# A graph layer's start and end: table stored in pieces, preparation less far ahead, sums in two banks, division on ScalarE

## The reference

```
w_m = (efeat @ W_msg + b_msg).reshape(E, 16, 16)
w_a = (efeat @ W_attn + b_attn).reshape(E, 16, 16)
e1 = w_m * x[src][:, :, None];  e2 = w_a * x[src][:, :, None]
ex = exp(e2 - segment_max(e2, dst)[dst])
ft = segment_sum(e1 * ex / segment_sum(ex, dst)[dst], dst)
out = layernorm(x + ft.sum(axis=1))
```

## Time and profile before

| what | us |
|---|---|
| median of 3 runs | 1687.11 (1686.28 to 1688.92) |
| the profiled execution, its own time | 1689.2 |
| its span, first to last instruction | 1687.1 |
| PE, DVE, ACT, POOL busy | 1308.6, 1514.4, 987.8, 966.8 |
| span of the loop by the shifts of tiles 0 and 109 | 179.77 to 1547.51 |
| the nodes' five pieces on DVE | 1618.34 to 1678.02 |

### The profile page before, as it was taken

How to read it: one execution, slowest core, us unless ns; L and a number is a source line. 1 busy time by engine, 2 the same in 40 slices (tenths; PEclk the granted TensorE clock), 3 DMA queues, 4 the chain that set the end, 5 groups by cost and what they waited for, 6 DMA issues and landing times. The chain is left out here.

```text
span 1687.1 us, 20610 instructions
## 1 busy us (share of the span) xinstructions
PE 1308.6 (78%) x5657; PEld 675.5 (40%) x5657; DVE 1514.4 (90%) x1504; ACT 987.8 (59%) x2062; POOL 966.8 (57%) x878
## 2 busy tenths in 40 slices
PE   0002799999999999999999999999999999998300
PEld 0001444444444444444444444444444444443200
DVE  8623899999999999999999999999999999998368
ACT  1002567767767767777777677677676666664100
POOL 5777777777676767677677777676770000000170
PEclk9999899999999999999999999999999999999655
DMA  4314344444444444444444444444443223221250
GB/s 109 81 19 106 89 131 122 128 128 118 133 125 115 132 126 119 128 125 119 130 122 124 129 118 131 125 116 133 125 118 115 88 79 99 84 75 51 62 149 15
DMA packets 175870, 182.93 MB, mean 108 GB/s; under 512 B 48376, under 2 KB 131208, under 8 KB 175758
## 3 DMA queue, kind: packets, MB, share of 16 engines
q1 hardware_dynamic: 141838, 158.74, 30.0%
q0 software_dynamic: 33920, 22.89, 9.5%
HBM read 92.36 MB, written 89.41 MB: 108 GB/s over the span
## 5 line engine op out<-in xcount | busy, mean ns | idle before, releaser
L490 POOL DMA_INDIRECT split<-x_parts,edge_src x784 | 873.1, 1114 | 321.5 <-issue 221.6
L797 PE MATMUL bank_sum<-em,row_onehot 128*128 128x512 f32 x1760 | 861.6, 602 | 31.0 <-ACT sum_rows L661 31.0
L1031 DVE TENSOR_TENSOR em<-bank_prod,h_rows 128x1024 f32<-128x1024 f32 x440 | 515.7, 1213 | 41.8 <-issue 32.6
L797 PEld LDWEIGHTS bank_sum<-em,row_onehot 128*128 128x128 f32 x1760 | 307.5, 189 | 269.4 <-issue 235.2
L1049 DVE TENSOR_TENSOR em<-em 128x1024 f32<-128x1024 f32 x220 | 267.8, 1218 | 3.5 <-ACT em L620 3.5
L785 PE MATMUL bank_prod<-w_rows,partsT 100*128 100x512 bf16 x880 | 269.5, 388 | 1.5 <-DVE em L1031 1.5
L1074 DVE TENSOR_TENSOR em<-em,bank_max 128x2048 f32<-128x2048 f32 x110 | 250.7, 2279 | 3.2 <-ACT node_max L652 3.2
L661 ACT COPY sum_rows<-bank_sum 128x512 f32<-128x512 f32 x220 | 126.6, 576 | 176.6 <-PE bank_sum L797 176.6
L620 ACT ACTIVATE em<-em 128x2048 f32<-128x2048 f32 x110 | 210.5, 1913 | 1.5 <-DVE em L1074 1.4
L644 ACT COPY chunk_fwd<-bank_max 128x512 f32<-128x512 f32 x110 | 64.5, 586 | 238.0 <-PE bank_max L727 238.0
L490 POOL DMA_INDIRECT em<-sums,rec_from_i x4 | 4.0, 992 | 305.2 <-DMA sums<-sum_rows 304.3
(11 more groups left out here) (166 smaller groups left out, 1214.6 us busy)
## 6 DMA issues: line engine op xcount, KB each, us to landing
sums<-sum_rows SPq DMA_DIRECT2D x110, 512.0 KB, 3.0
rec<-split_records SPq DMA_DIRECT2D x220, 144.0 KB, 2.2
split_records<-split SPq DMA_DIRECT2D x97, 288.0 KB
mask<-tile_table SPq DMA_DIRECT2D x110, 192.0 KB, 3.3
split<-x_parts,edge_src POOLq DMA_INDIRECT x784
rel<-tile_table SPq DMA_DIRECT2D x110, 64.0 KB, 3.0
edge_feat<-in_features SPq DMA_DIRECT2D x97, 64.0 KB
flag<-tile_table SPq DMA_DIRECT2D x110, 2.0 KB
```

The costliest lines, as they stand in the source:

```text
L490: return nc.gpsimd.indirect_dma_start(out, None, src, bass.IndirectOffsetOnAxis(idx, 0))
L797: mm = nc.tensor.matmul(bank_sum[:, :], row_onehot[:, t % RING, g, :], em[:, t % RING, s * GROUPS + g, :, :, :].rearrange("p i m o -> p (i ...
L1031: V.tensor_tensor(em[:, v, 2 * j:2 * j + 2, :, :, :].rearrange("p s i m o -> p s i (m o)"), bank_prod[j % 2][:, :, :].rearrange("p s (i x) ...
```

## The change

- **Table.** `c_tab` is stored in three pieces, `rel` first, then flags, then masks; DVE computes them in this order, with a semaphore for each. SP loads the records of tiles 0 and 1 and the flags of tile 0 between the pieces, ahead of the loop; the masks' piece stands in iteration -2. The record table is stored in iteration 0 and loaded in iteration 2, before both were earlier. The transposed row counts use `bank_sum`, and `base_row` is copied as soon as it is turned.
- **Preparation.** PREP_FIRST is 4 and not 6, so LEAD is 8. The loads of preparations 5 and 6, which stood ahead of the table's load on SP, now stand in iterations -4 and -3.
- **Last sums.** The second group of tiles 108 and 109 goes to `bank_t[1]`, and the waits for the copies allow one group more.
- **Nodes.** ACT computes a guess exp(-ln(s)) of each 1/s; DVE makes s*guess and m*guess and then (s*guess - 2)*(m*guess), which is -m/s after one Newton step; the mask for nodes is negated. ACT runs a first Sqrt on one element behind the last Exp.

```diff
-PREP_FIRST = 6
+PREP_FIRST = 4
+        def sums_bank(t, g):
+            return bank_t[1] if t >= TILES - 2 and g == 1 else bank_sum
...
             store_prep(0)
-            load_prep(5)
             store_prep(1)
-            load_prep(6)
...
-            sp.wait_ge(chunk_ready, 1)
-            sp.dma_start(tab_d, c_tab[:, :]).then_inc(tab_stored, 16)
...
-            for q in range(2, PREP_FIRST - 2):
-                store_prep(q)
+            sp.wait_ge(rel_ready, 1)
+            sp.dma_start(tab_d[:, 3 * WIDE:4 * WIDE], c_tab[:, 3 * WIDE:4 * WIDE]).then_inc(rel_stored, 16)
...
+            load_records(0)
+            sp.wait_ge(flags_ready, 1)
+            sp.dma_start(tab_d[:, 4 * WIDE:8 * WIDE], c_tab[:, 4 * WIDE:8 * WIDE]).then_inc(flags_stored, 16)
+            load_records(1)
+            load_flags(0)
             for t in range(FIRST, LAST + 1):
                 load_prep(q + 1)
-                load_records(t + 4)
+                if t + 4 > 1:
+                    load_records(t + 4)
+                if t == -2:
+                    sp.wait_ge(masks_ready, 1)
+                    sp.dma_start(tab_d[:, 0:3 * WIDE], c_tab[:, 0:3 * WIDE]).then_inc(masks_stored, 16)
...
+            for c in range(5):
+                act.wait_ge(f_loaded[c], 80)
+                guess = f_guesses[0:NODE_P, c % 2, :, :, :]
...
+                since(act, f_used, c - 1)
+                nc.scalar.activation(guess, whole[:, :, :, 0, :], ACT.Ln).then_inc(f_log, 1)
+                act.wait_ge(f_log, c + 1)
+                nc.scalar.activation(guess, guess, ACT.Exp, scale=-1.0).then_inc(f_guess, 1)
+            nc.scalar.activation(f_stat[:, 3, 0:1], eps[:, :], ACT.Sqrt)
...
-                    since(pe, sums_copied, 2 * t + g)
+                    since(pe, sums_copied, 2 * t + g - 1 if t >= TILES - 1 or (t == TILES - 2 and g == 1) else 2 * t + g)
                 for s in slots:
-                    mm = nc.tensor.matmul(bank_sum[:, :], row_onehot[:, t % RING, g, :],
+                    mm = nc.tensor.matmul(sums_bank(t, g)[:, :], row_onehot[:, t % RING, g, :],
...
             for c in range(5):
-                v_eng.wait_ge(f_loaded[c], 80)
-                link(V.reciprocal(sums_of(c, 0), sums_of(c, 0)))
-                link(V.tensor_tensor(sums_of(c, 1), sums_of(c, 1), sums_of(c, 0), ALU.mult))
+                v_eng.wait_ge(f_guess, c + 1)
...
+                link(V.tensor_tensor(sums_of(c, 0), sums_of(c, 0), guess, ALU.mult))
+                link(V.tensor_tensor(sums_of(c, 1), sums_of(c, 1), guess, ALU.mult))
+                link(V.scalar_tensor_tensor(out=sums_of(c, 1), in0=sums_of(c, 0), scalar=2.0, in1=sums_of(c, 1),
+                                            op0=ALU.subtract, op1=ALU.mult))
```

More of the change, by code:

```diff
@@ L128, in gnn_kernel @@
         has_edges = sb("has_edges", [P, NODE_COLS])
+        minus_edges = sb("minus_edges", [P, NODE_COLS])
         table = sb("table", [TILES, WIDE, COLUMNS])
@@ L224, in gnn_kernel @@
         fin = region(0, NODE_COLS, BOTH)
+        guess_at = NODE_COLS * BOTH
+        f_guesses = em_flat[:, guess_at:guess_at + 10 * ATT].rearrange("p (u n i o) -> p u n i o", u=2, n=5, i=FEAT)
         iotas = sem("iotas")
@@ L240, in gnn_kernel @@
         ends_ps = sem("ends_ps")
-        chunk_ready = sem("chunk_ready")
+        rel_ready = sem("rel_ready")
+        negrow_ready = sem("negrow_ready")
+        flags_ready = sem("flags_ready")
+        masks_ready = sem("masks_ready")
+        records_ready = sem("records_ready")
         chunk_ps = sem("chunk_ps")
+        base_copied = sem("base_copied")
         chunk_cols = sem("chunk_cols")
-        tab_stored = sem("tab_stored")
+        rel_stored = sem("rel_stored")
+        flags_stored = sem("flags_stored")
+        masks_stored = sem("masks_stored")
         rectab_stored = sem("rectab_stored")
@@ L308, in gnn_kernel @@
         f_loaded = [sem(f"f_loaded{c}") for c in range(5)]
+        f_log = sem("f_log")
+        f_guess = sem("f_guess")
         f_used = sem("f_used")
@@ L407, in load_records @@
                 q = min(t, PREPS - 1)
+                sp.wait_ge(base_copied, 1)
                 sp.wait_ge(split_stored[q % PREP_RING], rounds(q, PREP_RING))
@@ L421, in load_flags @@
                 w = t % 2
+                sp.wait_ge(flags_stored, 16)
                 since(sp, h_ready, t - 1)
@@ L452, in _ @@
                 if t == 0:
+                    sp.wait_ge(records_ready, 1)
+                    for k in range(4):
+                        sp.dma_start(rectab_d[k, :].rearrange("(t r) -> t r", r=4),
+                                     c_rec[:, k, :]).then_inc(rectab_stored, 16)
+                if t == 2:
                     sp.wait_ge(rectab_stored, 64)
@@ L573, in _ @@
                 part3(q - 2)
-            act.wait_ge(chunk_cols, 3)
             def row_places(t):
@@ L579, in row_places @@
                     return
+                act.wait_ge(chunk_cols, 2)
                 since(act, sums_ready, 2 * (t - RING + 1))
@@ L660, in copy_sums @@
                     act.wait_ge(rows_stored[v], 16 * (t // OUT_RING))
-                nc.scalar.copy(sum_rows[:, v, g, :], bank_sum[:, :]).then_inc(sums_copied, 1)
+                nc.scalar.copy(sum_rows[:, v, g, :], sums_bank(t, g)[:, :]).then_inc(sums_copied, 1)
             for t in range(FIRST, LAST + 1):
@@ L686, in _ @@
             nc.scalar.activation(r_weight[:, :, :], r_shift[:, :, :], ACT.Exp).then_inc(r_exp, 1)
+            for c in range(5):
+                act.wait_ge(f_loaded[c], 80)
+                guess = f_guesses[0:NODE_P, c % 2, :, :, :]
+                whole = fin[0:NODE_P, 5 * c:5 * c + 5, :].rearrange("p n (i m o) -> p n i m o", m=2, o=FEAT)
+                since(act, f_used, c - 1)
[3 more added lines that the diff above has]
+            nc.scalar.activation(f_stat[:, 3, 0:1], eps[:, :], ACT.Sqrt)
             act.wait_ge(f_var, 1)
@@ L908, in _ @@
             V.tensor_copy(w_part[:, 2, :], w_rest[:, :]).then_inc(w_split, 1)
-            for q in range(PREP_RING):
+            for q in range(PREP_FIRST - 1):
                 rest1(q)
@@ L921, in _ @@
             link(V.tensor_tensor(has_edges[:, :], start[:, 1:COLS], start[:, 0:NODE_COLS], ALU.is_gt))
+            link(V.tensor_scalar(minus_edges[:, :], has_edges[:, :], -1.0, None, ALU.mult))
             link(V.tensor_scalar(tmp[:, :], start[:, :], 1.0, 0.0, ALU.subtract, ALU.max))
@@ L964, in _ @@
             link(V.tensor_copy(tile_carry[:, :], bank_max[0:TILES, 128:128 + COLUMNS]))
-            link(V.tensor_scalar(c_node[:, :], filled[:, 0, :], tile_carry[:, 0:1], None, ALU.max))
             link(V.tensor_scalar(c_off[:, :], filled[:, 1, :], tile_carry[:, 1:2], None, ALU.max))
-            link(V.tensor_scalar(c_begin[:, :], filled[:, 2, :], tile_carry[:, 2:3], None, ALU.max))
             link(V.tensor_tensor(c_blk[:, :], chunk_iota[:, :], c_off[:, :], ALU.subtract))
             link(V.tensor_scalar(c_blk[:, :], c_blk[:, :], float(NUM_BLOCKS - 1), None, ALU.min))
[L970 to L974, removed]
+            link(V.tensor_scalar(c_base[:, :], c_blk[:, 0:WIDE:P], float(LAST_BASE), None, ALU.min))
+            V.tensor_tensor(c_tab[:, 3 * WIDE:4 * WIDE].rearrange("t (g j) -> t g j", g=GROUPS),
+                            c_blk[:, :].rearrange("t (g j) -> t g j", g=GROUPS), bc(c_base[:, :], 2, [TILES, GROUPS, P]),
+                            ALU.subtract).then_inc(rel_ready, 1)
+            v_eng.wait_ge(rel_ready, 1)
+            link(V.tensor_scalar(c_begin[:, :], filled[:, 2, :], tile_carry[:, 2:3], None, ALU.max))
             link(V.tensor_tensor(c_at[:, :], c_begin[:, :], c_group[:, :], ALU.max))
-            link(V.tensor_tensor(c_negrow[:, :], c_group[:, :], c_at[:, :], ALU.subtract))
+            V.tensor_tensor(c_negrow[:, :], c_group[:, :], c_at[:, :], ALU.subtract).then_inc(negrow_ready, 1)
+            v_eng.wait_ge(chunk_ps, 1)
+            V.tensor_copy(base_row[:, :], bank_t[0][0:GROUPS, 0:TILES]).then_inc(base_copied, 1)
             for col, out in ((3, c_first), (4, c_end)):
@@ L984, in _ @@
                 link(V.tensor_scalar(c_a[:, :], c_first[:, :], float(k), None, ALU.is_gt))
-                link(V.scalar_tensor_tensor(out=c_tab[:, (4 + k) * WIDE:(5 + k) * WIDE], in0=c_end[:, :], scalar=k + 0.5,
-                                            in1=c_a[:, :], op0=ALU.is_lt, op1=ALU.add))
+                flags = V.scalar_tensor_tensor(out=c_tab[:, (4 + k) * WIDE:(5 + k) * WIDE], in0=c_end[:, :], scalar=k + 0.5,
+                                               in1=c_a[:, :], op0=ALU.is_lt, op1=ALU.add)
+                if k < SLOTS - 1:
+                    link(flags)
+            flags.then_inc(flags_ready, 1)
+            v_eng.wait_ge(flags_ready, 1)
+            link(V.tensor_scalar(c_node[:, :], filled[:, 0, :], tile_carry[:, 0:1], None, ALU.max))
             link(V.tensor_tensor(c_a[:, 1:WIDE], c_node[:, 1:WIDE], c_node[:, 0:WIDE - 1], ALU.not_equal))
```

(2 more changed lines are left out.)

29 lines of the change are left out of this document (13 added, 16 removed).

## The result

The change made the kernel faster. The median of four runs is 1649.72 us (1646.35 to 1650.12), against 1687.94 of the kernel before in the same comparison (1686.28 to 1688.92): a ratio of 0.977, 95% interval 0.9753 to 0.9787. The forecast was 1649 in 1641 to 1658. The profiled execution took 1650.12, its span 1648.2, so 38.9 us less span than before.

The account below looks back on a forecast made before the run. Bounds: PE and DVE in the loop, POOL's preparations at the start, DVE's reciprocals at the end. Gains 19.0 + 3.0 + 16.1 = 38.1 off 1689.2 give 1651.1, less 2.1 for the median: 1649, range 1641 to 1658.

Parts of the forecast that it names:

- The tile does not change: Loop over the tiles: PE and DVE keep 12.57 us a tile, and two preparations moved into it cost nothing.
- The start, 19.0: Before tile 0's shift: shorter lead and table in three pieces bring it from 179.77 to 160.8, 19.0 us, range 15 to 21.
- store_prep(5) waits for POOL, about 150.7: SP's iteration -1: the store of preparation 5 waits for POOL until about 150.7; tile 2's flags end at 151.8.
- the prediction's two ways: Tile 0's shift: 159.5 counted from tile 2's flags, 160.3 to 161.3 over tile 1's flags and the forward scan.
- The sums, 3.0: Last sums in two banks: three boundaries lose their wait, 1.0 us each, 3.0 us; lower bound 2.3.
- The tail, 16.1: Node pieces: POOL's gathers become the bound in place of DVE; end at 1661.9 against 1678.0, 16.1 us.
- the gathers' delay: Tail: nine DVE two-input operations fall on POOL's gather issue and delay it 0 to 3.4 us, 2.5 taken.
- the last landing: Tail: 5.78 us from the fifth gather's start to landing, taken from the first piece, puts piece 4 at 1648.6.
- Rival 1: Start: it does not move, as a piece's landing or preparation 5's late load can hold the flags; 1668, chance 0.08.
- Rival 2: Tail: each gather waits for a whole DVE two-input operation, three pieces 13.4 us late in place of 2.5; 1660, chance 0.08.
- Rival 3: Loop: the shorter lead makes every tile wait; at 0.5 us a tile the time is 1704, chance 0.03.
- the terms' own bounds: Ranges behind 1641 to 1657: start 15 to 21, sums 2.3 to 3.2, tail 13 to 20 us.

Follow-up runs that it names:

- the faster version: Changed kernel with flags of tiles 1 and 2 moved ahead on SP, no Newton step, node pieces of 6, 6, 6, 4 and 3: 1642.29 us.
- the kernels that took one half back: Changed kernel with preparation six tiles ahead again (PREP_FIRST 6), 1668.03 us; changed kernel with the table stored whole ahead of everything, 1655.2 us.
- the part alone: Kernel before with only the second bank for the last sums added: 1685.17 us, ratio 0.998, against 1688.4.

## Why the prediction was right

- **The tile does not change.** Forecast 12.57, measured 12.57 with a lead of 10, 8 and 7. The two preparations more in the loop cost nothing.
- **The start, 19.0.** Measured 18.9 at tile 0 and 18.6 at tile 109. In detail, part3(3) was forecast for 136.5 and SP stored at 136.50; flags of tile 1 for 145.2 and ended at 145.82; flags of tile 2 for 151.8 and ended at 152.62; the shift for 160.8 and came at 160.86. One name was wrong: "store_prep(5) waits for POOL, about 150.7". SP went on when ACT's part3 was done, at 151.56, with POOL close by: where ACT is earlier, the landing of POOL's gathers releases store 5, at 151.89 with tile 1's flags moved and at 150.80 in the faster version. That 0.9 us did not reach the shift, since DVE had no gap from 149.71 to it: of the prediction's two ways, 159.5 over tile 2's flags and 160.3 to 161.3 over tile 1's, the second decided, and the 160.8 taken lies in it. The lead is what mattered most, as the steps had it: taken back, 18 us go.
- **What was not weighed:** the start was given as one term of 19. Its halves don't add, 11.5 + 0.8 against 18.9. This was shown only by the kernels that took one half back, and my expectation for the one with the table whole was 3.7 us off.
- **The sums, 3.0.** Measured 3.3 to the first gather and 3.2 by the part alone; the starts 3.43 to 3.51 apart for 3.44.
- **The tail, 16.1.** Measured 17.0. Mis-sized were the gathers' delay (2.5 taken; 38.45 - 36.34 = 2.1 against the trace of before) and the last landing (5.78 taken, 5.26). Ln and Exp were 1.27 for 1.26, the load on the path 1.28, the scalar_tensor_tensor 1.50 for 1.49, the last piece on DVE 6.88 for 6.87.
- **Rival 1 (start does not move), 0.08:** refuted for the change by 160.86. The kernel with the longer lead gives its time, 1668.03 for 1668, but there SP waits for POOL's gathers and not for what the rival named.
- **Rival 2 (exclusion on POOL), 0.08:** DVE does hold up POOL's gathers, shown by the kernel with DVE held back, but by 2.5 us and not 13.4. The forecast's price from four operations in the loop, 0.38 us each, was the right scale. By the rule of the Trainium skill (SBUF — State Buffer, SBUF: two separate sides) a gather stands for the whole of an operation. In this trace the gather of 2.49 looks like that, but most gathers beside such operations keep 1.18 to 1.24, so the trace does not bear the rule out for them. Why one is held up and the next isn't stays open.
- **Rival 3 (shorter lead costs every tile), 0.03:** refuted by the shifts of the change and of the kernel with a lead of 7.
- The Trainium skill (ScalarE: Activation LUTs, What ACT_TABLE_LOAD costs) adds a drain of 1.38 to a load. The Exp starts 0.01 us after the load ends here, and taking the load away gives 1.29 us. Its section on table sets has ln and exp in one set; in this program a load stands between them each time, five so, and five more ahead of a Ln.
- **The sum.** Part of the agreement is luck. The profiled execution gained 38.9 us in its span for 38.1 forecast, 0.8 more. But the 2.1 us by which the median lay under the profiled execution before were only 0.4 after the change, which takes back 1.7. So the median came out 0.7 above the forecast. The lower end of the range was also mis-added: by the terms' own bounds the greatest gain is 21 + 3.2 + 20 = 44.2, which gives 1643 and not 1641. The measured time is inside either way.

Not tried: tile 2's flags ahead of store 5 without the other changes of the faster version, and the preparation gathered earlier by POOL, which is the next limit of store 5. The fill of tiles 0 to 4 varies from kernel to kernel between 50.4 and 51.9 us, and no run was made for it.

## What to carry to other kernels

A queue that issues in order makes everything behind it wait for its slowest client: look what stands ahead of the first tile's inputs, and how far ahead of its use it is. When several things hold up the start, taking one away can look worthless until the other is gone, so test them in pairs. An operation moved to an idle engine gives time only until the next producer, here POOL's gathers, becomes the bound. After that, work taken off counts only in the last piece, between its landing and its end, and a smaller last piece shortens that too.

## What the runs showed of the hardware

- A gather issued by POOL beside DVE's operations with two SBUF inputs is mostly undisturbed (1.18 to 1.24 us), and now and then takes 1.3 to 2.5. From the first gather to the last it was 36.6 to 38.6 us in ten executions with the division on ScalarE (two of them without the Newton step, one with Exp for Ln), 36.34 beside the reciprocals before, and 35.95 with DVE held back. Against that one execution the delay is 0.7 to 2.6 us, and it differs between executions of the same kernel (38.45 and 36.68 for the change).
- Ln followed by Exp loads a table between them, and the next Ln loads one again; in the changed kernel the load for the next Ln starts as soon as Exp has ended, while ACT still has to wait for the gathers to land (load at 1600.19, Ln at 1603.66), so it adds nothing. It does not pass every wait: with DVE held back, the load for the third Ln came only at 1632.53, behind the wait for DVE's sum.
- TensorE goes from one bank to the other without a gap: 3.43 us from group to group of eight matmuls.
